# A batch's residual made by ScalarE inside the FFN's turn instead of by VectorE behind the router's norm

## What is computed

```python
x = L0_attn_a_x                                   # (8, 512, 128)
x = x + attn_a(layernorm(x))
x = x + ffn(layernorm(x))                         # FFN 1, router 1
x = x + attn_b(layernorm(x))                      # state-space layer
x = x + ffn(layernorm(x))                         # FFN 2, router 2

def ffn(x):                                       # x is already layer-normed
    t = x * rsqrt(mean(x * x) + EPS) * scale
    g = t @ gate_w.T + gate_b
    vals, idx = top_k(g, 4)
    route = one-hot sum of softmax(vals)          # (tokens, 16 experts)
    acc = sum over experts e: route[e] * (swiglu(t @ w1[e].T + b1[e]) @ w2[e].T + b2[e])
    return x + acc
```

## Time and profile before

| | before |
|---|---|
| median of 3 runs | 730.05 us (729.69 to 730.87) |
| the profiled execution: its own time | 729.9 us |
| its span | 728.2 us |
| attention loop, F1, state-space loop, F2 (first silu or matmul of each, us from the start) | 0, 119, 310, 531 |
| PE, DVE, ACT, POOL busy, share of the span | 97%, 86%, 79%, 33% |
| granted TensorE clock over the span | 1.00 |

### The profile page before, as it was taken

One profiled execution on the slowest core, in us unless ns is written; L12 is line 12 of the kernel. 1 busy time (PEld: TensorE's weight loads), 2 busy tenths in 40 slices (PEclk: granted clock), 3 DMA queues, 4 the chain that ended last, 5 costly groups with the idle time before them and its releaser, 6 DMA issues. The chain is left out here.

```text
span 728.2 us, 13033 instructions
## 1 busy us (share of the span) xinstructions
PE 707.1 (97%) x3800; PEld 575.9 (79%) x3800; DVE 626.2 (86%) x1503; ACT 573.4 (79%) x1095; POOL 243.4 (33%) x389
## 2 busy tenths in 40 slices
PE   6899999999999999999999999999999999999998
PEld 4688787888788877778888888888778887887886
DVE  3578886999999999967689999899769989998996
ACT  2676777988988899767787787787678889888885
POOL 2355464000015200015767767767740000610000
PEclk9999999999999999999999999999999999999999
DMA  9000012654555445400000000000146555654651
GB/s 273 5 2 3 9 33 88 219 196 156 179 188 193 166 167 180 140 0 2 1 1 1 4 3 1 9 4 1 32 174 211 177 196 190 199 196 168 224 195 53
DMA packets 29380, 77.19 MB, mean 106 GB/s; under 512 B 4899, under 2 KB 9726, under 8 KB 29310
## 3 DMA queue, kind: packets, MB, share of 16 engines
q1 hardware_dynamic: 28980, 76.29, 30.8%
q10 hardware_dynamic: 330, 0.08, 0.1%
HBM read 73.73 MB, written 2.62 MB: 105 GB/s over the span
## 5 line engine op out<-in xcount | busy, mean ns | idle before, releaser
L707 ACT ACTIVATE s_ring<-ps,b1T 128x512 f32<-128x512 f32 x256 | 171.5, 688 | 34.6 <-PE ps L1695 33.4
L1168 DVE SCALAR_TENSOR_TENSOR s_ring<-s_ring,top_col,r_all 128x1024 f32<-128x1024 f32 x128 | 166.0, 1297 | 18.4 <-ACT s_ring L707 17.8
L1180 DVE TENSOR_TENSOR s_lo<-s_ring,s_hi 128x1024 fp32r<-128x1024 f32 x126 | 153.8, 1220 | 3.8 <-ACT s_hi L713 3.8
L713 ACT ACTIVATE s_hi<-s_ring 128x1024 fp32r<-128x1024 f32 x128 | 135.1, 1055 | 9.3 <-DVE s_ring L1168 8.4
L1669 PE MATMUL ps<-s_hi,w_hi 128*128 128x512 f32 x256 | 101.5, 397 | 1.8 <-DVE s_lo L1180 1.7
L1693 PE MATMUL ps<-ffn_hi,w_hi 128*128 128x512 f32 x256 | 103.3, 404 | 0.0
L1671 PE MATMUL ps<-s_hi,w_lo 128*128 128x512 f32 x256 | 101.3, 396 | 0.0
L1695 PE MATMUL ps<-ffn_hi,w_lo 128*128 128x512 f32 x256 | 101.1, 395 | 0.0
L1694 PE MATMUL ps<-ffn_lo,w_hi 128*128 128x512 f32 x256 | 101.0, 395 | 0.0
L1670 PE MATMUL ps<-s_lo,w_hi 128*128 128x512 f32 x256 | 100.8, 394 | 0.0
L523 POOL TENSOR_TENSOR ramp<-upto,dt_a 128x512 f32<-128x512 f32 x32 | 33.0, 1043 | 83.0 <-PE ps L1671 71.5
(11 more groups left out here) (263 smaller groups left out, 1550.5 us busy)
## 6 DMA issues: line engine op xcount, KB each, us to landing
r_all<-route_dram SPq DMA_DIRECT2D x128, 512.0 KB, 3.8
out_dram<-X SPq DMA_DIRECT2D x7, 256.0 KB, 4.3
X<-in_L_attn_a_x_dram SPq DMA_DIRECT2D x1, 1536.0 KB, 9.5
rows_f<-route_dram SPq DMA_DIRECT2D x48, 32.0 KB, 2.9
w_rows<-in_L_ffn_mlp_w_dram SPq DMA_DIRECT2D x1, 1024.0 KB, 6.8
route_dram<-route_cols SPq DMA_DIRECT2D x64, 8.0 KB, 1.5
X<-in_L_attn_a_x_dram SPq DMA_DIRECT2D x2, 256.0 KB, 4.9
ssm_rows<-in_L_attn_b_W_in_dram SPq DMA_DIRECT2D x1, 384.0 KB
```

The costliest lines, as they stand in the source:

```text
L707: eng.activation(s_ring[q % NR][:, e % 2, :], bank(e % 4), ACT.Silu, bias=b1T[:, e:e + 1], scale=ALPHA).then_inc(F["act"], 1)
L713: eng.activation(s_hi[q % NR][:, :, :], s_ring[q % NR][:, :, :], ACT.Copy).then_inc(F["hi"], 1)
L1168: eng.scalar_tensor_tensor(out=s_ring[q % NR][:, :, :], in0=s_ring[q % NR][:, :, :], scalar=top_col[:, 0:1], in1=r_all[q % NR][:, :, :], o ...
L1180: eng.tensor_tensor(s_lo[q % NR][:, :, :], s_ring[q % NR][:, :, :], s_hi[q % NR][:, :, :].bitcast(F32), ALU.subtract).then_inc(F["lo"], 1)
```

## The change

`router_xn` goes away. ScalarE gets `residual(R, b)`, four activations of 128x128 (Identity with a column as scale and a column as bias, in place in `X`), in `late_router` at pair 1 of batch b, for all eight batches of both FFN stages. Its two columns are kept per batch in a new buffer `res_col`, which `router_chain` writes: 1 + r directly, and -m * r in three operations where one made m * r. The chain grows from nine to eleven operations. `router_norm` waits for the seventh of them instead of the ninth. Two waits are new on VectorE: `bn_aggr` waits for the whole chain of the batch before, and `add_sum` waits for the batch's `residual`. The chain waits for `t0` of the batch before instead of for `router_xn`. A staging row `vec_row` is laid into `attn` for its space.

```diff
@@ router_chain (GpSimd)
-                    wait(eng, R["pool"], 9 * b + n[0])
+                    wait(eng, R["pool"], 11 * b + n[0])
...
-                wait(eng, R["xn"], NT * b)
+                wait(eng, R["t0"], NT * b)
...
-                tt(rt_small[:, 7, :], rt_small[:, 1, :], ones[:, 0:NT], ALU.add)
-                eng.tensor_tensor(rt_small[:, 8, :], rt_small[:, 1, :], rt_mv[:, :, 0], ALU.mult).then_inc(R["pool"], 1)
+                tt(res_col[:, b, 0, :], rt_small[:, 1, :], ones[:, 0:NT], ALU.add)
+                tt(rt_small[:, 7, :], rt_small[:, 1, :], mhalf4[:, :], ALU.mult)
+                tt(rt_small[:, 8, :], rt_small[:, 7, :], rt_mv[:, :, 0], ALU.mult)
+                eng.tensor_tensor(res_col[:, b, 1, :], rt_small[:, 8, :], rt_small[:, 8, :], ALU.add).then_inc(R["pool"], 1)
@@ ScalarE
+            def residual(R, b):
+                eng.wait_ge(R["pool"], 11 * (b + 1))
+                eng.wait_ge(R["t0"], NT * (b + 1))
+                for r in range(NT):
+                    eng.activation(X[:, b, r, :], X[:, b, r, :], ACT.Identity, bias=res_col[:, b, 1, r:r + 1],
+                                   scale=res_col[:, b, 0, r:r + 1]).then_inc(R["xn"], 1)
...
             def late_router(R, F, b, q):
+                if q == 1 and b < NB:
+                    residual(R, b)
@@ VectorE
+                wait(eng, R["pool"], 11 * b)
                 for r in range(NT):
                     eng.bn_aggr(rt_mv[:, r, :], rt_st[:, r, :]).then_inc(R["aggr"], 1)
...
-                wait(eng, R["pool"], 9 * b + 9)
+                wait(eng, R["pool"], 11 * b + 7)
...
-            def router_xn(R, b):
-                eng.wait_ge(R["t0"], NT * b + NT).then_inc(passed, 1)
-                for r in range(NT):
-                    eng.tensor_scalar(X[:, b, r, :], X[:, b, r, :], rt_small[:, 7, r:r + 1], rt_small[:, 8, r:r + 1],
-                                      ALU.mult, ALU.subtract).then_inc(R["xn"], 1)
...
             def add_sum(F, b, at):
                 wait(eng, F["back"], b + done(F) + 1)
+                eng.wait_ge((R1 if F is F1 else R2)["xn"], NT * (b + 1))
```

More of the change, by code:

```diff
@@ L68, in build @@
         gate_rows = sb("gate_rows", [NE, D])
-        vec_row = sb("vec_row", [1, 160])
         scale_col = sb("scale_col", [P, 1])
@@ L93, in build @@
         rt_small = sb("rt_small", [P, 9, NT])
+        res_col = sb("res_col", [P, NB, 2, NT])
         t0 = sb("t0", [P, NT, D])
@@ L137, in build @@
             attn = own("attn", [P, NT, D])
+            vec_row = attn[:, 0:2, :].rearrange("p r d -> p (r d)")[0:1, 0:160]
             neg_max = own("neg_max", [P, NT])
@@ L1322, in late_router @@
                     router_norm(R, NB - 2)
-                elif (b, q) == (1, 6):
-                    router_xn(R, NB - 2)
                 elif (b, q) == (2, 2):
@@ L1338, in late_router @@
                     router_weights(R, NB - 1)
-                elif (b, q) == (6, 2):
-                    router_xn(R, NB - 1)
             def ffn_all(R, F):
@@ L1387, in step @@
                     router_norm(R1, i - 1)
-                    router_xn(R1, i - 1)
                 if not first:
@@ L1460, in step @@
                     router_norm(R2, i - 2)
-                    router_xn(R2, i - 2)
                 if second:
@@ L1526, in _ @@
                 wait(eng, F2["back"], 2 * NB + half)
+                eng.wait_ge(R2["xn"], NT * NB)
                 rows = slice(2 * half, 2 * half + 2)
```

## The result

The changed kernel takes 744.13 us (median of 5 runs, 743.45 to 745.73) beside 729.72 us for the kernel before (729.50 to 730.87): 1.0188 times as long, 95% interval 1.0168 to 1.0208. Slower was forecast, but by 6.35 us, and it is 14.4; 744.13 lies 5 us above the upper end of the range. The profiled execution has a span of 742.4 us against 728.2, a granted clock of 1.00 in both, so the two traces hold the whole difference.

A forecast was written before the change was run, and what follows sets the result against it. PE's work was taken to set the pace, other engines mattering only where PE waits for them last. The terms -0.45 + 3.3 + 3.5 = +6.35 us gave 736.4 us, range 731.5 to 739.0.

The forecast's parts named there:

- ScalarE's work is absorbed in 11 batches of 16: FFN stages: the four added activations, 1.56 us per batch, fit ScalarE's idling in 11 batches, costing 0 us.
- The five tight batches: F1 batches 0, 5, 6 and F2 batches 0, 5: ScalarE lacks room, so the activations cost +3.5 us.
- The price of an activation: ScalarE in each FFN batch: bounded from other rows at 0.50 us per activation, 1.56 us for four.
- rival 3: FFN batches: the activations are short, 1.04 us for four, total 734.1 us; chance 0.13.
- rival 5: FFN batches: the activations are long, 2.0 us for four, total 738.5 us; chance 0.09.
- GpSimd's two operations: SSM steps 1 to 6: two more chain operations delay PE by 0.55 us a step, +3.3 us.
- Step 7: SSM loop, step 7: with router_xn gone cb is ready earlier and a PE wait ends, -0.45 us.
- The work taken from VectorE is worth nothing elsewhere: Attention loop, SSM steps 2 to 6 and FFN stages: removing router_xn from VectorE gains 0 us.
- Rival 1: SSM loop: VectorE bounds it, so six removed blocks of 1.12 us count and POOL's operations vanish, 726.9 us; chance 0.09.
- The rest: New waits, the vector row moved into attn, and ACT's table loads: 0 us.

The follow-up runs named there:

- run 1: The changed kernel with the four activations behind pair 3 instead of pair 1 of each FFN batch: 740.67 us, ratio 1.0146.
- run 2: The changed kernel with two of the four activations behind pair 1 and two behind pair 3: 739.23 us, ratio 1.0119.
- run 11: The changed kernel with the buffers back at the addresses of the kernel before, nothing else: 743.74 us, ratio 1.0170.
- run 3: The changed kernel with the residual made by VectorE at the old places, chain of eleven kept: 735.76 us, ratio 1.0072.
- run 4: The changed kernel with the chain's last four operations, which make the two columns, at the end of GpSimd's step in the state-space loop ("columns late"): 739.95 us, ratio 1.0122.
- run 12: As run 10, but with the residual on VectorE at its old places: 730.27 us, ratio 0.9985.
- run 10: The changed kernel with columns made late in GpSimd's step, activations where ScalarE idles, and buffers at the old addresses: 729.18 us, ratio 0.9970.
- run 7: The kernel before, unchanged, run and traced once more (the second trace of before): 731.12 us, ratio 1.0004.
- the first run under 9: The kernel before with only its buffers moved, first of two runs: 731.81 us, ratio 1.0003.

## Why the forecast was wrong, step by step

**ScalarE's work is absorbed in 11 batches of 16: this step failed.** It counted 0.69 and 0.89 us of idling "further on in the batch" and 0.44 ahead of the next silu as room for 1.56. But room counts only up to the first thing on that engine for which PE waits. The 0.69 and 0.89 lie behind pairs 3 and 4 and so behind the copy of bank 6; ahead of it there are 0.44 of idling and 0.36 of slack. The view of waits was read for `s_lo` alone; `b_st` had next to no idle time before, and that was taken as "nobody waits" when it meant "just in time". By the two rows ahead of the copy the sum would have been 1.54 - 0.80 = 0.74 in an ordinary batch; the batches show 0.65, of which 0.57 is left with the buffers in their old place (23.61 against 23.04). Runs 1 and 2 show the mechanism, in dose too. The eleven batches forecast at 0 are +7.4 together (6.8 in run 11, with the buffers in their old place). The whole forecast missed by 7.9 us.

**The five tight batches, +3.5 forecast and +2.0 measured: the mechanism held in two of them, in the other three PE waits elsewhere.** F1 batch 0 was forecast at +1.03 and is +0.92, F2 batch 0 at +0.33 and is +0.35. In F1 batch 0 it shows as the wait for `s_lo`, against the slack of the earlier trace rows:

```profile
134.40 1.22 DVE L1187 TENSOR_TENSOR s_lo<-s_ring,s_hi 128x1024 fp32r<-128x1024 f32 x1
135.67 0.19 PEld L1672 LDWEIGHTS ps<-s_hi,w_hi 128*128 128x128 f32 x1 [1.01 <-DVE s_lo L1187]
```

The three batches with table loads (F1 batches 5 and 6, F2 batch 5) were forecast at +0.38, +1.12 and +0.61 and are +0.01, +0.68 and +0.03. In all three the new wait is that for the copy at `b_st`, 0.6 to 0.7 us, and what PE waits for once it does not wait for again. F1 batch 6 has nothing but this wait, and its old wait for `s_lo` (0.5) is unchanged. In F2 batch 5 the two old waits for `s_lo`, 0.37 and 1.17 us, became one of 0.77 and so took the new one in; F1 batch 7 (+0.04) hides it in the same way. The step added delays to old waits as if they were independent. F1 batch 5 is a case of its own: against the second trace of before it is +0.41, near the +0.38 forecast, but by luck, since that forecast counted 0.37 us of idling ahead of `s_hi` that the second trace does not have, and named another wait.

**The price of an activation was right.** 487 ns against an estimate of 0.50 us, 1.54 us for four against 1.56. The estimate of 0.29 us from the table in the Trainium skill ("VectorE: DVE Perf Modes", the section on the TRN2 errata) is 0.2 too low for an activation with two columns; rivals 3 and 5 have no part in the result.

**GpSimd's two operations, 6 x 0.55 = +3.3: right in mechanism, low by 0.85.** `state` is again 0.1 us behind `state_d` in all six steps, and steps 2, 3, 4 and 6 are longer by 0.53 to 0.60. Step 5 has 0.75, and step 1 has 1.20: there the chain's second power took 1.54 us instead of 1.01, and `bn_aggr` came 0.36 us later in the step than in the trace of before. Step 1 is +1.2 in all four traced kernels that have the chain whole and the residual on ScalarE; with the residual on VectorE (run 3) it is +0.44, and steps 2 and 3 are +0.9. The same long power and late `bn_aggr` are in the five traces with the columns late and the residual on ScalarE, where step 1 is +0.2. So it isn't chance, but what it is stays open. Runs 3 and 4 show the cause from both sides: with the longer chain and without ScalarE's work the loop is +4.1, and with the columns out of the way the cost is gone.

**Step 7, -0.45: right.** It is -0.46 at the load of `xs`, and 0.14 more behind it.

**The work taken from VectorE is worth nothing elsewhere: right but for one place.** Rival 1 (VectorE bounds the loop) falls: steps 2 to 6 won 0.07 us each when both GpSimd and VectorE had less ahead. But run 12 against run 10 has 0.9 us in the loop: 1.1 us in step 7, nearly all of it ahead of the load of `xs`, less the 0.2 of step 1.

**"The rest", 0: wrong twice.** The vector row's move was priced by who reads it and when; it also moved every weight and ring in SBUF, the on-chip memory. That is 0.8 us of the 14.2 (run 11 against the changed kernel), and 1.5 in a kernel without the wait. And 0.33 us come at the end of the attention loop in every kernel with the residual on ScalarE: VectorE's softmax of the router then meets GpSimd's `rows_r`, one of its small operations takes 0.59 us where it took 0.23, and PE waits 0.39 us for `rt_w`, for which it did not wait. The 0.98 before 22 us are no effect of the change: up to there the traces differ from the first one of before by -0.35 to +1.27, and a second trace of before by 1.02.

Together: 1.0 from the start, 0.3 and 0.8 from "the rest", 3.5 for the loop against 2.85, and 8.6 for the FFN at old addresses against 3.5, which is 14.2.

## What to carry to other kernels

When work is put into an engine's stream, look for the first instruction behind it on which the bounding engine waits, and count idle time and slack only up to there; that engine's lack of a wait before may be exactly in time. Put such work behind that instruction, not ahead of it: here other places for the activations, the columns at the end of the step and the old addresses turned 14 us lost into 2 us won (run 10). And a small operation on an engine that runs in order costs what stands behind it, so what is needed late goes to the end of the step.

## What the runs showed of the hardware

- **Where buffers lie changes a matmul's time.** A batch of 96 matmuls of 512 columns without waits takes 23.04 us with the weights and rings at their old addresses or 256 bytes lower, and 23.17 to 23.19 with them 384 lower, or the weights 640 and the rings 384. All 16 traces fall on the one or the other side by this. Four layouts fit a step of 256 bytes; that it is 256 and not something coarser or finer was not tried further, nor which operand does it.
- **TensorE's clock fell in some executions and not in others of the same program,** each time behind a stretch in which PE had waited. Five of the 16 traces have it around 329 us, at the start of the state-space loop, where PE waits some 1.6 us for `xb_tok` (0.81 over the 9 us of run 7, so part of them at 1.2 GHz and the rest at 2.4 GHz; the first trace of before has 1.00 there), and run 4 has it at 23 us, behind a wait of 2.11 us; PE was busy 2.73 of the 4.8 us ahead of the fall (the window of the fall, granted clock 0.54, columns as in run 7):

```profile
22.80:26.50 3.70, 3.67 (x19) 3.70 (x20) 1.77 (x3) 2.04 (x4) 3.70 (x7) 0.54 0.00 0
```

One such fall goes with 1.2 to 2.9 us more, as much as the differences that the last runs were after, so stages were compared and not spans.
- **VectorE's operations can take far longer beside GpSimd's:** 1.36 us against 0.33 for one of four `tensor_scalar` (2.13 against 1.10 for the four), 1.54 against 0.70 for `gram`, 0.59 against 0.23 for a small one. How the two meet can differ between executions of one kernel: a multiply took 2.03 us in one and 1.56 in the other, and that moved a stage by 0.4 us.
- **TensorE alone can be slow in one execution:** of ten of the first run under 9, one took 2790 us, with matmuls at 1.1 us instead of 0.40 and VectorE's and ScalarE's operations as long as elsewhere. What caused it is open.
